# Loading and rounding the shared weights and FFN inputs of the last four blocks while the last expert tiles run

## The reference

```python
def relu2(x):
    r = jax.nn.relu(x)
    return r * r
...
    h1 = jnp.einsum('th,ehi->tei', x, w_up)
    a = relu2(h1) * combine[:, :, None]
    routed = jnp.einsum('tei,eih->th', a, w_down)
    shared = relu2(hidden_states @ shared_up) @ shared_down
    return routed.reshape(orig_shape) + shared
...
    x = x + _layernorm(_L0_attn_ref(_layernorm(x, axis=-1), ...), axis=-1)
    x = x + _layernorm(_L0_ffn_ref(_layernorm(x, axis=-1), ...), axis=-1)
```

## Time and profile before

| | us |
|---|---|
| median of 3 runs | 1610.94 (1610.04 to 1611.3) |
| the profiled execution | 1610.72 |
| its span, first to last instruction | 1608.9 |
| PE busy | 1508.8 (94%) |
| DVE busy | 966.2 (60%) |
| ACT busy | 782.8 (49%) |
| POOL busy | 807.6 (50%) |
| mean granted TensorE clock, of full speed | 0.976 |

### The profile page before, as it was taken

How to read it: one execution, slowest core, us unless ns; L and a number is a source line. 1 busy time by engine, 2 the same in 40 slices (tenths; PEclk the granted TensorE clock), 3 DMA queues, 4 the chain that set the end, 5 groups by cost and what they waited for, 6 DMA issues and landing times.

```text
span 1608.9 us, 21774 instructions
## 1 busy us (share of the span) xinstructions
PE 1508.8 (94%) x7006; PEld 1026.4 (64%) x7006; DVE 966.2 (60%) x1871; ACT 782.8 (49%) x1417; POOL 807.6 (50%) x828
## 2 busy tenths in 40 slices
PE   4599999999999999999999999997999999979997
PEld 2265666656666667566664677875666666657886
DVE  3466776767676776767667336841333333339998
ACT  2155657566565674665647354431222222265554
POOL 1056778697776977777779440013222222033341
PEclk9789999999999999999999999999999999989999
DMA  4848859499595895966954332509977777496773
GB/s 119 133 68 139 128 92 190 81 173 175 90 172 110 131 199 71 188 133 110 230 73 106 131 131 76 180 23 298 286 216 210 222 209 218 145 346 213 235 234 124
DMA packets 162759, 257.76 MB, mean 160 GB/s; under 512 B 20084, under 2 KB 70132, under 8 KB 160596
## 3 DMA queue, kind: packets, MB, share of 16 engines
q1 hardware_dynamic: 142472, 204.46, 56.5%
q0 software_dynamic: 14064, 46.02, 9.7%
q10 hardware_dynamic: 6112, 5.90, 1.2%
HBM read 103.74 MB, written 58.46 MB: 101 GB/s over the span
## 4 chain that ended last, share of the span: by engine, by line
PE 75%; DMA 8%; DVE 6%; ACT 4%; issue 4%; POOL 2%; SPq 2%; DVEq 0%; POOLq 0%; ACTq 0%
PE bank L113 11%; PE bank L708 9%; PE bank L776 9%; PE bank L799 8%; PE bank L730 7%; DMA a<-a 7%; PE bank L629 7%; PE bank L615 6%; PE bank L645 6%; PE bank L634 6%; PE bank L654 2%; PE bank L788 1%; ACT a L1347 1%; SPq L1756 1%; POOL a L1593 1%
## 5 line engine op out<-in xcount | busy, mean ns | idle before, releaser
L1593 POOL TENSOR_TENSOR a<-a 128x512 f32<-128x512 f32 x384 | 496.5, 1321 | 96.1 <-ACT a L1404 55.2
L1404 ACT ACTIVATE a<-bank 128x512 f32<-128x512 f32 x512 | 295.1, 598 | 241.5 <-PE bank L634 190.5
L909 DVE TENSOR_REDUCE a<-bank 128x1 f32<-128x512 f32 x512 | 323.2, 680 | 74.4 <-PE bank L615 73.4
L113 PE MATMUL bank<-a 128*128 128x512 f32 (+1 forms) x864 | 236.3, 398 | 6.2 <-DVE a L855 4.0
L629 PE MATMUL bank<-a 128*128 128x512 f32 x512 | 221.8, 433 | 6.2 <-ACT a L1404 5.8
L634 PE MATMUL bank<-a 68*128 68x512 f32 x512 | 205.6, 402 | 0.4 <-ACT a L1394 0.2
L113 PEld LDWEIGHTS bank<-a 128*128 128x128 f32 (+1 forms) x864 | 159.5, 187 | 53.3 <-issue 10.3
L708 PE MATMUL bank<-c 128*128 128x512 f32 x768 | 181.2, 396 | 13.1 <-ACT c L1452 6.9
L615 PE MATMUL bank<-a 128*128 128x512 f32 x512 | 176.2, 422 | 15.8 <-DMA a<-a 9.2
L1661 POOL DMA_INDIRECT f<-h_scratch,f x79 | 75.8, 960 | 222.8 <-DMA f<-f 192.9
L730 PE MATMUL bank<-c 128*128 128x512 f32 x768 | 178.0, 391 | 4.5 <-DVE c L967 2.1
(11 more groups left out here) (187 smaller groups left out, 1764.4 us busy)
## 6 DMA issues: line engine op xcount, KB each, us to landing
a<-a SPq DMA_DIRECT2D x272, 256.0 KB, 8.4
f<-f SPq DMA_DIRECT2D x316, 64.0 KB
yp_scratch<-f SPq DMA_DIRECT2D x79, 256.0 KB
a<-in_L_attn_x SPq DMA_DIRECT2D x15, 1024.0 KB, 8.7
x_scratch<-a SPq DMA_DIRECT2D x8, 1024.0 KB, 5.0
h_scratch<-a SPq DMA_DIRECT2D x8, 1024.0 KB, 10.3
hT_scratch<-s SPq DMA_DIRECT2D x8, 1024.0 KB, 9.4
c<-hT_scratch SPq DMA_DIRECT2D x8, 1024.0 KB, 7.1
```

Of the source, the lines that this page charges most:

```text
L113: t = e.matmul(out, a[n], b[n], start=n == 0 and m == 0, stop=n == len(ah) - 1 and m == 2)
L909: e.tensor_reduce(K.mx[:, i, j:j + 1], K.MX[n % 3][:], AX.X, ALU.max).then_inc(Z.max, 1)
L1404: e.activation(K.pt[:, n % NP, :], K.SC[n % 2][:], ACT.Exp, scale=SCALE).then_inc(Z.exp, 1)
L1593: e.tensor_tensor(K.acc[:, j, :], a, K.pt[:, n % NP, :], ALU.add).then_inc(Z.acc, 1)
```

## The change

It does five things.

- **Loads earlier.** `reload` is split. `reload up` (SP) stands behind the store of tile 73 and waits for `ed` 74: from then on no tile is of expert 9 or 10, whose places (0 and 1) `su2` takes. `reload h` and `reload down` stand behind the store of tile 75; the first waits until the last tile has been turned, the second for `ed` 76 (experts 11 and 12, places 2 and 3).
- **Rounds earlier.** `round up` 0 to 3 stand on ACT behind the copy of tile 76, `split h` of block 4 and `round up` 4 and 5 behind that of tile 77, `round up` 6 and 7 behind that of tile 78. `passed` is gone; DVE's `split h` waits instead for the last turn and the stores of tiles 72 and 73, and ACT's `up` for the stores that lie where it writes `aTh`.
- **Buffers.** `eyo` is rotated so that the `fso` buffers hold tiles 72 and 73 and not 77 and 78.
- **Rounds of the down weights** in block 4 come one step earlier (behind up 1 rather than up 2).
- **Gathers.** The first eight no longer wait for the weights: SP's wait for `ed` 79 alone, POOL's for `ed` 79 and the stores. The input of block 5 (`next h`) is loaded behind these eight on SP, as before.

```diff
+OVER = {LAST - 5: [("reload up",)], LAST - 3: [("reload h",), ("reload down",)], LAST - 2: [("round up", i) for i in range(4)],
+        LAST - 1: [("split h", FIRST, k) for k in range(4)] + [("round up", 4), ("round up", 5)], LAST: [("round up", 6), ("round up", 7)]}
...
             out.append(("e down", i - 3))
+        out += OVER.get(i - 3, [])
...
-    out = [("reload",)] + [("gather", n) for n in range(R)]
+    out = [("gather", n) for n in range(R)] + [("next h",)]
...
-    K.eyo = [K.fso[:, 0, :], K.fso[:, 1, :]] + [K.faT[:, k, :] for k in (0, 1, 2, 6, 7)]
+    K.eyo = [K.faT[:, 6, :], K.faT[:, 7, :], K.fso[:, 0, :], K.fso[:, 1, :]] + [K.faT[:, k, :] for k in (0, 1, 2)]
...
-        elif n >= 4:
-            w.wait_ge(Z.sd2, 16)
-        else:
-            w.wait_ge(Z.su2[3], 16)
...
+    def reload_up():
+        w.wait_ge(Z.ed, 64 + max(e_ for e_ in range(E) if PLACES[e_] < 2))
+        for n in range(4):
+            cut = slice(2 * n * P, 2 * (n + 1) * P)
+            e.dma_start(K.su2[:, :, cut], w_("L0_ffn_shared_up")[:, :, cut]).then_inc(Z.su2[n], 16)
+
+    def reload_h():
         w.wait_ge(Z.h_lo, 4 * FIRST)
         w.wait_ge(Z.hTs, 16 * (FIRST + 1))
         w.wait_ge(Z.hTt, NTILE)
         e.dma_start(K.raw, K.hT_d[FIRST]).then_inc(Z.hT, 16)
-        w.wait_ge(Z.ed, NTILE)
...
-        w.wait_ge(Z.su2[3], 16)
+
+    def reload_down():
+        w.wait_ge(Z.ed, 64 + max(e_ for e_ in range(E) if PLACES[e_] in (2, 3)))
         e.dma_start(K.sd2, w_("L0_ffn_shared_down")).then_inc(Z.sd2, 16)
```

More of the change, by code:

```diff
@@ L240, in shared_order @@
     fresh = b in (0, FIRST)
-    ups, downs = ("split up", "split down") if b == 0 else ("round up", "round down")
+    downs, late = ("split down", 2) if b == 0 else ("round down", 1)
     out = []
-    if b == FIRST:
-        out += [("split h", b, k) for k in range(4)] + [(ups, 0)]
     for i in range(8):
-        if b == FIRST and i + 1 < 8:
-            out.append((ups, i + 1))
         out.append(("up", b, i))
-        if fresh and i >= 2:
-            out.append((downs, i - 2))
+        if fresh and i >= late:
+            out.append((downs, i - late))
         out += step(i)
     if fresh:
-        out += [(downs, 6), (downs, 7)]
+        out += [(downs, i) for i in range(8 - late, 8)]
     if b + 1 < B and b + 1 != FIRST:
@@ L953, in split_h @@
         if b == FIRST:
-            w.wait_ge(Z.ed, NTILE)
+            w.wait_ge(Z.eT2, NTILE)
+            for n in (2, 3):
+                w.wait_ge(Z.yps[n], 16 * ((LAST - n) // 7 + 1))
         w.wait_ge(Z.h_hi, 4 * b + k + 1)
@@ L1439, in begun @@
             w.wait_ge(Z.stack[u % RS], 8 * 16 * (u // RS + 1))
-    def passed():
-        w.wait_ge(Z.ed, NTILE)
-        for i in range(LAST - 6, LAST + 1):
-            w.wait_ge(Z.yps[i % 7], 16 * (i // 7 + 1))
     def split_h(b, k):
-        if b == FIRST:
-            passed()
         w.wait_ge(Z.hT, 16 * (b + 1))
@@ L1801, in sync_program, with next_h @@
     w_ = lambda n: ins[n].rearrange("(k p) n -> p k n", p=P)
+    def next_h(b):
+        w.wait_ge(Z.h_lo, 4 * (b + 1))
+        w.wait_ge(Z.hTs, 16 * (b + 2))
+        e.dma_start(K.raw, K.hT_d[b + 1]).then_inc(Z.hT, 16)
     def split_h(b, k):
-        if k == 3 and b + 1 < B and b + 1 != FIRST:
-            w.wait_ge(Z.h_lo, 4 * (b + 1))
-            w.wait_ge(Z.hTs, 16 * (b + 2))
-            e.dma_start(K.raw, K.hT_d[b + 1]).then_inc(Z.hT, 16)
+        if k == 3 and b + 1 < B and b != FIRST and b + 1 != FIRST:
+            next_h(b)
     def over():
@@ L1897, in sync_program @@
               "early hT": early_hT, "load sd": load_sd, "split h": split_h, "weights": weights, "prepare": prepare, "move": move, "e down": e_down,
-              "choose early": choose, "reload": reload, "gather": gather, "finish": finish}
+              "choose early": choose, "reload up": reload_up, "reload h": reload_h,
+              "reload down": reload_down, "next h": lambda: next_h(FIRST), "gather": gather, "finish": finish}
     for name, *at in K.order:
```

18 lines of the change are left out of this document (6 added, 12 removed).

## The result

| | us |
|---|---|
| before, median of 20 executions beside it | 1612.4 (1609.51 to 1616.28) |
| the change, median of 20 executions | **1606.71** (1600.06 to 1612.19) |
| ratio, 95% interval | 0.9965 (0.9954 to 0.9976) |
| the profiled execution of the change | 1610.24, span 1608.4 |

Faster by 0.35%, or 5.7 us, where 15.0 were forecast: the sign is right, the size is not, and the measured time lies above the range of 1590.5 to 1602.5. (Of the 11.0 us between 1595.7 and 1606.71, 1.5 are the base: the median of before was 1610.94 over 3 executions and is 1612.4 over 20.) Two things stand out already. The times of the change spread over 12 us, those of before over 7. And the profiled execution is one of the slow end of that spread, so its profile shows what the median holds only in part.

A forecast was written before the change was run, and what follows sets the result against it. PE was taken as the bound, DVE next. PE's loss would fall from 20.0 us to 1.3 + 2.3 + 1.4 = 5.0, a gain of 15.0: span 1593.9 plus 1.82 gives 1595.7 us, range 1590.5 to 1602.5.

The forecast's parts named there:

- The bound and the bill of 20 us: PE bounds the kernel and loses 20.0 us between the last expert tile and its end, the most recoverable.
- The weights: Before and in block 4, the earlier up and down weight loads land hidden; ACT's 5.44 us down-cast wait goes.
- the lateness less some 3 us: Price in block 4 if the down weights land late: their lateness minus some 3 us.
- The input, 5.0 us: Block 4's input load lands 5.0 us after issue, at 1405.1, the queue being nearly empty; bounds 5.0 and 16.4.
- the forecast's 1.3: PE's loss at block 4's start: up 0 ends at 1409.75, 1.3 us late, with under 1 us of idle.
- I add nothing: At block 4's restart, no half-clock charge, since PE's idle stays under 1 us.
- one slow spell: Rival: PE starts block 4 sparsely, cast by cast, and the clock falls, costing 2.0 us; 1597.7, 9%.
- PE waits in down 0 for DVE's subtraction, 2.3 us: In block 4, up 7's last subtraction follows three adds, ending near 1436.3; down 0 wants it at 1434.0.
- S: DVE's first add, behind up 3's subtraction: forecast at 1420.5 against 1434.19 before, with gathers landing by 1420.2.
- late landings: Rival: gathers take 7.5 us (1598.4) or the input takes 9.2 with a slow spell (1601.9); about 1600, 16%.
- PE waits 1.4 us in block 5: At block 5's down 0, PE waits 1.4 us for DVE, because tile 19's add begins 4.8 us behind PE.
- A lag up to 3.4 is free: Tile 19's add may begin up to 3.4 us behind PE without costing PE in block 5.

The follow-up runs named there:

- down_late: The change with block 4's down weights loaded behind the store of tile 78 instead of tile 75; 1606.59 us, ratio 0.9964, against look_again's 1601.55.
- look_again: The change unaltered, run and traced a second time; 1601.55 us, ratio 0.9925 to the kernel before.
- look_third: The change unaltered, third trace; 1600.46 us, ratio 0.9928 to the kernel before.
- look_fourth: The change unaltered, fourth trace, on the chip of set 3; 1609.64 us (1600.63 to 1612.18), ratio 0.9969 to the kernel before.
- look_fifth: The change unaltered, run again as the base of its set; 1601.02 us, ratio 0.9926 to the kernel before.
- look_sixth: The change unaltered, run again as the base of the last set; 1601.22 us, ratio 0.993 to the kernel before.
- downs_before: The change with block 4's last down cast moved ahead of the square root before it; 1599.4 us, ratio 0.9913, against look_third's 1600.46.
- plain_rows: The change with the first eight tiles' indirect gathers replaced by SP's plain loads of fixed rows; 1600.08 us against look_fifth's 1601.02, repeated 1599.84 against look_sixth's 1601.22.
- sets 1, 2, 4 and 5: Follow-up sets running the change and variants beside the kernel before, one chip per set, the first and last sharing theirs; the change measured 1600.46 to 1601.55 us.
- set 3: Follow-up set on another chip, with the change, raw_early again, raw_downs and light_dve beside the kernel before; the change measured 1609.64 us.
- light_dve: The change with last layer norm statistics over 64 of 512 columns, altering the computation; 1606.51 us, ratio 0.9957, against look_fourth's 1609.64.
- raw_early: The change with block 4's input loaded one tile earlier, behind tile 74's store; 1598.22 us against look_again's 1601.55, repeated 1606.38 against look_fourth's 1609.64.
- raw_downs: raw_early's earlier input load together with downs_before's earlier last down cast; 1606.88 us, ratio 0.9956, against look_fourth's 1609.64.

## Why the prediction was right, and where it was not

**The bound and the bill of 20 us: right.** The loss before was 20.0 us by the prediction's sum, and all that changed lies between X and the end of block 4; from there on every half block takes 21.76 us, but for 0.5 to 0.6 us that block 5 loses in some traces.

**The weights: right.** No ACT cast waits for the up weights (1407.00 follows the copy at once), and none for the down weights. The price named for late down weights, "the lateness less some 3 us", was tested by down_late: ACT 6.49 us late, so 3.5 by that rule, and PE waits 4.04.

**The input, 5.0 us: this step failed first.** It was issued at 1403.90 and landed at 1411.77, 7.9 us; in other traces 6.2 to 8.3. The prediction took 5.0 "since the queue is again nearly empty", and it wasn't. The four up loads were issued 6 to 7 us ahead, with two stores behind them, and their last piece landed at 1405.85, 2 us behind the input's issue. The 5.0 of the earlier trace rows was measured with one store ahead, and holds for that case. The bounds, 5.0 and 16.4, held it; the value taken from between them was the wrong one. ACT waits 2.13 us, PE 2.42, and 0.8 to 2.2 in the five later traces of the change; forecast was an idle under 1 us. The other part of the forecast's 1.3, the pace of the input casts, was right: 0.9 us wherever the clock stayed full.

**"I add nothing" for the clock: this step failed too.** The prediction put a fall of the clock only behind an idle of several us. These are the five traces of the change without the late signal; idles in down 0 are counted from start to start. The last column is the loss above that of traces whose recorded clock stays full in the same place (there it is 0.9 at the start, and 0.2 in down 0 beside the idles).

| trace | idle at the start | loss behind it in `up` 0 and 1 | idles in down 0 | slow clock at the start, in down 0 |
|---|---|---|---|---|
| look_again | 1.0 | 0.9 | 1.3 + 1.8 | none, 1.6 |
| look_third | 1.6 | 2.5 | 0.5 + 1.8 | 1.6, none |
| look_fourth | 1.5 | 2.5 | 0.5 + 1.8 | 1.6, none |
| look_fifth | 2.1 | 2.2 | 0.5 + 1.8 | 1.2, 1.6 |
| look_sixth | 0.8 | 0.9 | 1.3 + 1.8 | none, 2.9 |

Half clock costs 1.6 to 2.9 us in each, while the whole loss exceeds the forecast by 2.2 to 3.5 (7.2 to 8.5 against 5.0). The rest of the excess is the start's idle, the longer first wait in down 0 of two traces and, in look_again, the 1.1 us around `up` 7, less the 1.4 us of block 5 that mostly didn't come. Over all 19 traces with the new order the start divides cleanly: behind an idle of 0.19 to 1.01 us (six traces) the clock stayed full, behind 1.25 to 2.42 us (thirteen) it fell, 0.2 to 2.3 us after PE had begun again. In down 0 of the traces without the late signal and with the change's order of casts it fell in all four whose first idle was 0.7 us or more, and in two of the nine where it was shorter. Two stretches right behind equal waits, first of look_fifth, then of look_third:

```profile
1440.00:1442.00 2.00, 2.00 (x6) 1.54 (x6) 1.86 (x6) 1.72 (x3) 0.00 (x0) 0.50 0.83 272
```

```profile
1441.00:1443.00 2.00, 2.00 (x11) 1.64 (x10) 1.86 (x6) 1.78 (x4) 0.00 (x0) 1.00 0.87 285
```

Idles of 0.5 and 1.8 us with three matmuls between them, and in one trace six matmuls fit in the next 2 us where the other has eleven. The rival "one slow spell" (1597.7, 9%) had this mechanism and its place, "PE starts sparsely at 1406, waiting cast by cast"; its chance was far too small, and there are one or two spells. Its 2.0 us came from the earlier trace rows, where the pace of the input casts is part of them, which the 1.3 already held (0.9); a spell alone costs 1.2 to 2.9. The rule that the prediction cited from the Trainium skill ("TensorE: Matmul & The Clock Gate", "HAM oscillation — how this bites in real kernels") speaks of short bursts between waits for data, with waits of 3 to 5 us in its example. The traces agree that such bursts bring the clock down, and here shorter waits were enough. The sum by the rule (1597.7, a loss of 7.0) was the better one.

**PE waits in down 0 for DVE's subtraction, 2.3 us: size nearly right, by luck, and the engine wrong.** It measured 0.5 + 1.8 to 1.3 + 1.8 us in the five traces, for ACT's last two down casts. They stand behind square roots that wait for DVE's statistics, so DVE sets the pace at one remove. The prediction followed DVE's order and not ACT's. downs_before shows DVE's own wait behind it, 1.0 us.

**The gathers and S: late by 3 us.** The first gather was forecast at X + 8.7 (1414.5) and came at X + 9.0 to 10.0 in the traces of the change; the first add was forecast at X + 14.7 and came at X + 17.5 to 18.5. In look_again and look_sixth DVE waits for the rows (2.96 and 2.15 us), which take some 7 us and not the 4.5 taken; that was the rival "late landings". In the other four traces of the change it doesn't wait: the add stands right behind the subtraction of `up` 3, which is late because PE is. It cost little: tile 19's add then lags PE by 0.8 to 3.6 us, below the 4.8 forecast, since PE is later too.

**PE waits 1.4 us in block 5: mostly wrong.** Block 5 loses 0.5 to 0.6 us where the lag is 3.5 us or more (look_third, look_fourth, plain_rows), and nothing where it is 2.1 or less. The loss stands in its `up` 6 and 7, where the one wait long enough to be listed is for ACT's relu, and not in its down 0. "A lag up to 3.4 is free" fits these traces; the lag forecast and the place don't.

**The late signals: not in the prediction at all, and the largest part of the miss.** In 22 executions of the change on the chips of sets 1, 2, 4 and 5 all times lie between 1599.35 and 1603.82. In the 32 of the first measurement and of set 3, 6 lie below 1603.82 and the rest go up to 1612.19. The kernel before has nearly the same median in all of them, 1612.4 to 1613.18. So the gain is 11.1 to 12.7 us where the signals are prompt, and 5.7 and 3.5 where they are not. Of the missing 9.3 us, some 3 are the two steps above, and about 6 are this. Where the signals are prompt, the medians (1600.46 to 1601.55) lie within the stated range, near its upper end. In the trace of before every recorded rise of this semaphore in block 4 stands at most 0.7 us behind the start of its matmul, and one trace can't show a spread, so the profile gave no row from which the late signals could have been priced. What holds PE's signals up is **open**: the traffic of POOL's indirect gathers, for which light_dve's trace speaks, full DMA engines, or something else of these chips. That the kernel before is spared is shown by its medians alone, and not explained.

The best variant on record is raw_early, 1598.22 (0.9913), and 1606.38 against 1609.64 on the chip of set 3. Against the before of its set (1612.66) that is a gain of 14.4 us; its start loses 1.1 us where the prediction had 1.3, and it keeps the slow spell in down 0.

## What to carry to other kernels

When a load is moved to a place just behind another large one, take its landing from the end of that one, not from a row in which it went first. Count a slow spell of the clock for a restart that goes piece by piece, even where the idle before it is only 1.3 to 2.4 us as here; better, bring the first operands one step earlier, which took the idle away here and left the clock full at the start in all three traces of it. Read the granted clock of the stretch before a loss is called slow clock: 0.9 us of this one were matmuls that waited for one cast each, at full clock. And where one execution is profiled but the times spread by more than the effect, profile a second one before a cause is named: the largest wait of the first profile was absent from the next five of the same kernel.

## What was not expected of the hardware

- The semaphore of a matmul rose 5.2 to 13.6 us after that matmul had begun, in four traces, instead of some 0.4, while the packets of indirect gathers moved (at 400 GB/s in all at first, at 230 in the longest wait of light_dve); in raw_downs PE issued single matmuls 1.2 to 2.8 us apart with nothing to wait for, and two signals 2.72 us apart were recorded 0.12 apart. One chip of four showed it, besides the first measurement, whose chip isn't known.
- Half clock came at the start behind idles of 1.25 to 2.42 us and never behind 1.01 or less, in 19 traces; behind 0.5 + 1.8 us in down 0 it came in one execution and not in another.
- A load of 1 MB took 7.9 us behind 2 MB of others, and its 16 parts ended from 1408.58 to 1411.77: the first reader waits for the slowest of them, 3.2 us behind the first.
